# Query, key and value projections of a gated block's second attention as three fp32r products; value copies on ScalarE; the last batch's weight transfers at other places

## The reference, cut to what matters

```python
q = (src @ Wq + bq).reshape(B, T, N_HEAD, HEAD_DIM)
k = (src @ Wk + bk).reshape(B, T, N_HEAD, HEAD_DIM)
v = (src @ Wv + bv).reshape(B, T, N_HEAD, HEAD_DIM)
scores = jnp.einsum('bqhd,bkhd->bhqk', q, k) * scale
probs = jax.nn.softmax(scores, axis=-1)
attn = jnp.einsum('bhqk,bkhd->bqhd', probs, v).reshape(B, T, D_MODEL)
attn = attn @ Wo + bo
x = _layer_norm(src + attn, ln1_g, ln1_b)
...
    h = jax.nn.relu(x @ W1[e] + b1[e])
    y = h @ W2[e] + b2[e]
```

## Time and profile before

| | us |
|---|---|
| median of three runs | 532.24 |
| lowest and highest | 523.12, 532.72 |
| the profiled execution | 519.03 |
| its span | 517.2 |
| mean granted clock of TensorE | 0.963 |

### The profile page before, as it was taken

How to read it: one execution, slowest core, us unless ns; L and a number is a source line. 1 busy time by engine, 2 the same in 40 slices (tenths; PEclk the granted TensorE clock), 3 DMA queues, 4 the chain that set the end, 5 groups by cost and what they waited for, 6 DMA issues and landing times. The chain is left out here.

```text
span 517.2 us, 8461 instructions
## 1 busy us (share of the span) xinstructions
PE 467.6 (90%) x2595; PEld 271.6 (53%) x2595; DVE 382.4 (74%) x835; ACT 249.3 (48%) x499; POOL 211.2 (41%) x286
## 2 busy tenths in 40 slices
PE   3989999999999999999998698999979999999980
PEld 2545443344344345344343233325469999999980
DVE  4554879788878989878979779934778766666661
ACT  2112206657453657344646555678145555555540
POOL 4254303312004412604401453854367556656652
PEclk9999999999998999998999979889999999999995
DMA  8628740752284652341763592011121211121220
GB/s 232 130 89 261 173 95 3 247 198 60 73 143 98 214 174 77 120 121 53 194 202 100 184 182 82 3 45 41 42 81 30 70 62 62 52 63 54 68 61 11
DMA packets 39854, 54.99 MB, mean 106 GB/s; under 512 B 12413, under 2 KB 24203, under 8 KB 39820
## 3 DMA queue, kind: packets, MB, share of 16 engines
q1 hardware_dynamic: 34096, 38.18, 28.0%
q0 software_dynamic: 5232, 15.93, 9.6%
q10 hardware_dynamic: 492, 0.47, 0.3%
HBM read 36.73 MB, written 17.83 MB: 105 GB/s over the span
## 5 line engine op out<-in xcount | busy, mean ns | idle before, releaser
L776 DVE TENSOR_REDUCE mx<-amax 128x1 f32<-128x512 f32 x256 | 166.1, 678 | 41.3 <-PE amax L934 41.1
L630 ACT ACTIVATE probs<-sc 128x512 f32<-128x512 f32 x232 | 128.7, 596 | 135.3 <-PE sc L946 132.7
L934 PE MATMUL amax<-KS,QS 48*128 48x512 f32 x256 | 101.8, 474 | 4.1 <-DVE mx L776 2.8
L946 PE MATMUL sc<-QS,KS 50*128 50x512 f32 x232 | 91.1, 465 | 12.4 <-ACT probs L630 8.2
L946 PEld LDWEIGHTS sc<-QS,KS 50*128 50x128 f32 x232 | 36.8, 189 | 99.1 <-ACT probs L630 51.4
L934 PEld LDWEIGHTS amax<-KS,QS 48*128 48x128 f32 x256 | 40.6, 188 | 21.5 <-DVE mx L776 14.6
L1379 PE MATMUL amax<-W_hi,hid_hi 128*128 128x256 f32 x160 | 46.1, 288 | 0.0
L1379 PE MATMUL amax<-W_lo,hid_hi 128*128 128x256 f32 x160 | 45.2, 283 | 0.0
L1379 PE MATMUL amax<-W_hi,hid_lo 128*128 128x256 f32 x160 | 45.2, 283 | 0.0
L556 POOL TENSOR_TENSOR an<-av,rec 128x256 f32<-128x256 f32 x16 | 10.2, 636 | 83.7 <-DVE rec L765 83.6
L1095 POOL DMA_INDIRECT out_dram<-slot_z,ids_now x22 | 27.3, 1240 | 28.9 <-DVE slot_z L1299 24.4
(11 more groups left out here) (264 smaller groups left out, 932.1 us busy)
## 6 DMA issues: line engine op xcount, KB each, us to landing
qk_dram<-HL SPq DMA_DIRECT2D x16, 512.0 KB, 4.5
QS<-qk_dram SPq DMA_DIRECT2D x90, 64.0 KB, 3.0
KS<-qk_dram SPq DMA_DIRECT2D x90, 64.0 KB, 2.9
W_sb<-in_L_ffn_W SPq DMA_DIRECT2D x8, 512.0 KB, 4.2
xc<-in_x SPq DMA_DIRECT2D x4, 512.0 KB, 3.5
xc<-in_ctx SPq DMA_DIRECT2D x4, 512.0 KB, 4.5
tok_dram<-xc POOLq DMA_DIRECT2D x4, 512.0 KB, 3.6
res_dram<-t_a POOLq DMA_DIRECT2D x4, 512.0 KB, 3.9
```

Of the source, the lines that this page charges most:

```text
L630: nc.scalar.activation(probs[:, n % 8, c * 512:(c + 1) * 512], score_bank(u)[:, :], ACT.Exp, scale=SCALE).then_inc(exp_done, 1)
L776: nc.vector.reduce_max(mx[:, to:to + 1], amax[m % 3][:, :], AX.X).then_inc(max_done, 1)
L934: nc.tensor.matmul(amax[m % 3][:, :], QS[rows, pair, chunk * P:(chunk + 1) * P], KS[rows, pair, :], start=True, stop=True).then_inc(A_full, 1)
L946: nc.tensor.matmul(score_bank(u)[:, :], KS[rows, pair, kc * P:(kc + 1) * P], QS[rows, pair, :], start=True, stop=True).then_inc(sc_full, 1)
```

## The change

- **Three products.** Wq, Wk and Wv are split once, in the lead-in: ScalarE writes three fp32r high halves `qkv_hi` ahead of xT, POOL six low halves `qkv_lo` behind `scale(0)`. `srcT` becomes fp32r, and VectorE writes `srcT_lo` from the transposes' bank, which is held until then (`sl_done`). A block of q or k is six fp32r matmuls of 512 columns, three per half; a half of v is six of 256 columns. The second half of q waits for `srcT_lo`.
- **Value copies.** ScalarE copies v into V1 without a bias. Since the probabilities of a query sum to one, the value bias is taken through Wo once and added to the row Bo: Bv is loaded in head order by four small DMAs on ScalarE's queue, transposed on TensorE, copied by ScalarE, multiplied with Wo in two matmuls and added by VectorE, all in the lead-in. POOL's first `residual` waits for it.
- **Loads.** Wq, Wk, Wv go ahead of the rows for all partitions, of which seven are left. `qkv_hi` and `srcT_lo` share memory with the W1 pieces of experts 2 and 3, which are therefore loaded once the last v is done; both tables of pieces get new units.
- **POOL.** Each low half of `split_early` is written as four quarters. In batches 0 and 1 the store of the expert input and the load of the next residual stand at units 125 and 130 in place of right behind the arithmetic.

```diff
+            with ExitStack() as shared:
+                shared.enter_context(nc.sbuf_tensor("W1_first", [P, 4, F], fp32))
+                srcT_lo = shared.enter_context(nc.sbuf_tensor("srcT_lo", [P, KD, S], fp32r))
+                qkv_hi = shared.enter_context(nc.sbuf_tensor("qkv_hi", [P, 3 * KD, D], fp32r))
             W1_sb = att("W1_sb", [P, E * KD, F])
...
-                 -44: ("q", 0), -41: ("q", 1), -39: ("k", 0), -36: ("k", 1)}
+                 -44: ("q", 0), -41: ("q", 1), -39: ("k", 0), -36: ("k", 1), -33: ("v", 0), -31: ("v", 1)}
...
-                  -43: (("q", 0),), -40: (("q", 1),), -38: (("k", 0),), -35: (("k", 1),), -33: (("v", 0),), -31: (("v", 1),),
+                  -48: (("sT", 0),), -47: (("sT", 1),), -43: (("q", 0),), -40: (("q", 1),), -38: (("k", 0),), -35: (("k", 1),),
...
-        GPSIMD = {-98: "ln0", -90: "bias", -59: "ln1", -53: "x1", -47: "residual", 80: "ln2", 113: "xf"}
+        GPSIMD = {-98: "ln0", -90: "bias", -59: "ln1", -53: "x1", -47: "residual", 80: "ln2", 113: "xf", 125: "xf_store", 130: "xf_next"}
...
-        FIRST_LAYERS = {14 + 14 * i: i for i in range(E * KD)}
+        FIRST_LAYERS = {14: 0, 28: 1, 42: 2, 56: 3, 211: 4, 216: 5, 229: 6, 233: 7}
...
-        SECOND_LAYERS = {144 + 10 * i: i for i in range(2 * E)}
+        SECOND_LAYERS = {144: 0, 147: 1, 197: 2, 206: 3, 221: 4, 225: 5, 237: 6, 241: 7}
...
-            for i, v in ((BO2, Bo), (BV, Bv), (G1, ln1_g), (B1, ln1_b), (RW, router_w.rearrange("d o -> (d o)")), (G2, ln2_g), (B2, ln2_b)):
+            for n, ap in (("Wq", Wq), ("Wk", Wk), ("Wv", Wv)):
+                load_weight(n, ap, qkv_loaded)
+            for i, v in ((BO2, Bo), (G1, ln1_g), (B1, ln1_b), (RW, router_w.rearrange("d o -> (d o)")), (G2, ln2_g), (B2, ln2_b)):
...
             scale(0)
+            for w in range(3):
+                pool.wait_ge(qkv_high, w + 1)
+                for k in range(KD):
+                    j = KD * w + k
+                    nc.gpsimd.tensor_tensor(qkv_lo[:, j, :], w_second[:, j, :], qkv_hi[:, j, :].bitcast(fp32), ALU.subtract).then_inc(qkv_split, 1)
             bias(0)
...
-                nc.gpsimd.tensor_tensor(low, whole, high.bitcast(fp32), ALU.subtract).then_inc(early_split, 1)
+                pool.wait_ge(early_split, 5 * EARLY.index((w, part)) + 1)
+                for q in range(4):
+                    low_q, whole_q, high_q = [quarter(t, q) for t in (low, whole, high)]
+                    nc.gpsimd.tensor_tensor(low_q, whole_q, high_q.bitcast(fp32), ALU.subtract).then_inc(early_split, 1)
...
+                elif task == "v":
+                    act.wait_ge(v_full, b * 2 + i + 1)
+                    nc.scalar.activation(V1[b % 2][:, 2 * i:2 * i + 2, :, 0:DH], bank[:, :].rearrange("p (t h d) -> p t h d", t=2, h=H), ACT.Identity).then_inc(v_done, 1)
...
+                if (task, i) == ("xT", 0):
+                    act.wait_ge(qkv_loaded, 3 * 16)
+                    for w in range(3):
+                        nc.scalar.activation(qkv_hi[:, KD * w:KD * (w + 1), :], w_second[:, KD * w:KD * (w + 1), :], ACT.Identity).then_inc(qkv_high, 1)
...
+                elif task == "sT":
+                    dve.wait_ge(sT_done, b * 2 + i + 1)
+                    nc.vector.tensor_tensor(srcT_lo[:, i, :], bank[:, :], srcT[:, i, :].bitcast(fp32), ALU.subtract).then_inc(sl_done, 1)
...
-                elif task == "v":
-                    dve.wait_ge(v_full, b * 2 + i + 1)
-                    nc.vector.tensor_tensor(V1[b % 2][:, 2 * i:2 * i + 2, :, 0:DH], bank[:, :].rearrange("p (t h d) -> p t h d", t=2, h=H),
-                                            rows_bc[:, BV:BV + 1, :].rearrange("p o (h d) -> p o h d", h=H).broadcast_to([P, 2, H, DH]), ALU.add).then_inc(v_done, 1)
...
+            for c in range(KD):
+                side_work("sT", c, 0)
+            dve.wait_ge(vb_full, 1)
+            nc.vector.tensor_tensor(rows_bc[:, BO2, :], BANKS[0][:, 0:D], rows_bc[:, BO2, :], ALU.add).then_inc(vb_done, 1)
             for v in V1:
                 nc.vector.memset(v[:, :, :, DH:2 * DH], 1.0).then_inc(v1_ready, 1)
...
+            def parts_features(bank, w, c, half, full):
+
+                steps = [(0, 0, 0), (0, 0, 1), (1, 0, 0), (1, 0, 1), (0, 1, 0), (0, 1, 1)]
+                for wp, xp, k in steps[3 * half:3 * half + 3]:
+                    last = nc.tensor.matmul(bank[:, :], w[wp][:, k, c * P:(c + 1) * P], (srcT, srcT_lo)[xp][:, k, :], start=((wp, xp, k) == steps[0]), stop=((wp, xp, k) == steps[-1]))
+                if half == 1:
+                    last.then_inc(full, 1)
...
-                    pe.wait_ge(sT_done, b * 2 + 2)
-                    features_out(bank, w_sb["W" + task], i, srcT, half, qk_full)
+                    pe.wait_ge((sT_done, sl_done)[half], b * 2 + 2)
+                    parts_features(bank, qkv_parts[task], i, half, qk_full)
```

100 lines of the change are left out of this document (73 added, 27 removed).

## The result

The changed kernel takes 546.57 us, the median of four runs (545.4 to 551.92); the kernel before took 527.68 us in the same rounds (522.97 to 532.72). The ratio is 1.047 with a 95% interval of 1.035 to 1.059: slower. (Ratios leave out every run more than 1.5% above the fastest of its kernel, so they are not the quotients of the medians.) I had said 521 us.

What follows compares the result with a forecast made beforehand. TensorE was taken to bound the projection stretches, with VectorE having little to spare. Lead-in +2.2, projections -4.4, last batch -3.2 and quarters 0 sum to -5.4 us, from 526.8 to 521 us; range 508 to 533.

Steps and rivals of the forecast that it cites:

- rival (d): Projections beside attention: short TensorE idle times bring eight more low-clock stretches, +8.2 us, 535 us; chance 0.15.
- The products: Projections on TensorE: fp32r products save 0.20 us per q or k half, 0.14 per v half, 2.2 us per batch.
- Rival (b): Projections: weight loads of the new products are not hidden, +2.2 instead of -4.4 us, 528 us; chance 0.08.
- VectorE swaps two value copies ... I take two thirds, 4.4 us: Projections of batches 1 to 3: VectorE will be late, so 4.4 of 6.6 us are gained, ends 2.0 and 6.6.
- The lead-in: Before the first scores: later xT and low half of q lose 2.2 us, ends 0 and 4.
- Rival (c): Lead-in: Wv lands at 22 us and projections come late, sum +0.6 us, 527 us; chance 0.08.
- The last batch: Last batch's transfers: no large load ahead of the maxima gains 3.2 us, ends 0 and 4.8.
- SP writes the maxima out at 289.51, behind ... a 512 KB load: Last batch: maxima wait behind twelve stack loads and a 512 KB load on SP; 4.4 us hang on it.
- nobody waits for POOL then: First two batches: moving POOL's store and residual load apart makes them wait 3.4 us at most, effect 0.
- ScalarE's copies: Projections: two more ScalarE evictions of about 0.60 us per batch cost nothing; 3.6 us lost if cover is gone.
- The quarters: POOL's low halves of weight splits written as four quarters: effect 0, ends -1.5 and +1.5 us.
- rival (a): Whole kernel: all gains come through and three low-clock stretches go, -16.5 us, 510 us; chance 0.17.

Runs made afterwards that it cites:

- e13: e10 with two W2 loads moved from units 171 and 173 to 187 and 188, and a third from 197 to 202: 529.5 us, ratio 1.004.
- e16: e13 with the products in fp32 of the high halves: 533.9 us, ratio 1.012.
- e1: The changed kernel with the three fp32r products replaced by one fp32 product of the high halves: 537.2 us, ratio 1.011.
- e10: The changed kernel with e5's lead-in, e9's wait on POOL, some KS loads issued earlier and three weight loads moved: 532.3 us, ratio 1.007.
- e5: The changed kernel with high halves made behind xT and gates, POOL's first bias ahead of its low halves, ScalarE's QS moves later: 539.0 us, 1.015 by the medians.
- e4: The kernel before with only the change's moved weight loads and their semaphore: 528.5 us, ratio 1.000.
- e9: The kernel before with POOL's FFN input store of batches 0 and 1 held until maxima two batches on are back in QS: 532.7 us, ratio 0.999.
- e17: e13 with the value copies on VectorE again, without the bias: 531.0 us, ratio 1.007.
- e18: e16 without VectorE's low halves of srcT and TensorE's wait for them: 531.6 us, ratio 1.003.
- e7: The kernel before with the second product of each q and k block over 256 of its 512 columns: 533.8 us, ratio 0.998.
- e11: The kernel before with the change's moved weight loads and e10's three edits to the transfers, not the lead-in: 537.3 us, ratio 1.024.

## Why the prediction was wrong

The forecast failed, and what came has rival (d)'s sign but not its mechanism. (d) had short idle times between the groups of products; what came is two waits of over 3 us for a transfer, a longer lead-in, and a clock that fell behind these and at other places as well. Its 8.2 us for eight more low stretches were too few: the changed kernel has 55 us more at the low clock, sixteen times 3.4.

**The products** were the right size: 0.79 us a half of q or k in place of 0.955 (1.58 and 1.91 for two), 0.81 in place of 0.96 for v, so 8 x 0.165 + 4 x 0.15 = 1.9 us a batch against my 2.2. (My 0.66 and 0.86 for a half were both too short, so the difference held.) Even the 4.4 us that I took for them is what e13 has over e16, in a kernel whose transfers had first been moved; that the number agrees is luck, since my two thirds were for VectorE's being late. Rival (b), loads that are not hidden, is refuted by the rows from 275.12 us.

**The step that failed** is "VectorE swaps two value copies ... I take two thirds, 4.4 us": I asked only whether TensorE or VectorE would bound the shorter stretch, and not what was timed against it. The way of k over DRAM was: q and k evicted, stored, landed, fetched in six loads, all paced by SP, VectorE and ScalarE, with the v blocks and four scores as its cover. In the earlier trace rows nothing shows it, nor do the waits at a batch's first maxima, because it was just covered. In the changed kernel the cover fell short by 3.65 and 3.31 us, idle time in which the clock dropped, and undoing the products alone gains 9.4 us in the medians (e1) and 3.6% by the ratios: the term has the wrong sign, and is off by some 14 us or more. That the short products do save where these waits are gone (e10, e13) shows that the step failed by the overlap and not by the products' price.

**The lead-in** (2.2, ends 0 to 4) cost 4.9 us in the profile, and e5 gives back some 7.6 by the medians. Wv landed near the late end of my range (xT at 19.00, I had said 17.8), the cover was 0.4 us and not 0.7, and I did not price the low clock behind TensorE's idle 2.83 us, 1.7 more: these two are the steps that failed here. My 0.4 us for the low half of q was right: 5.4 us late in all (41.86), of which srcT is 5.0. Rival (c), a landing at 22 us, did not happen.

**The last batch** (3.2, ends 0 to 4.8) is worth 0, give or take some 2.5 us (e4). The step that failed is "SP writes the maxima out at 289.51, behind ... a 512 KB load": I looked at SP's queue alone, and what slowed it was POOL's store at 288.85 us. I had even costed that store's move at 0, "nobody waits for POOL then", which was true of POOL and not of what it sends. And with the delay gone (e9) the time did not move, so the 4.4 us that I hung on it were too many as well. In the changed kernel the wait is still there, 2.81 us.

**ScalarE's copies** at 0 hold as far as e17 can tell. VectorE's low halves, which I had at nothing of their own, may cost up to some 5 us (e18). **The quarters** at 0 were not tried alone.

**The clock.** I gave (d) 0.15 because idle times of 0.45 us stand all over the last batches at full clock. Those were the wrong idle times to look at. What I had in the earlier trace rows was the right one: 2.42 us without work, and 6.8 us at 1.2 GHz behind it. My range began at 508, below rival (a)'s own 510, and ended at 533, short of (d)'s 535: the upper end is where more room was needed. The Trainium skill, TensorE: Matmul & The Clock Gate, section HAM oscillation — how this bites in real kernels, tells of a kernel whose clock fell after each wait for a DMA; the rows at 22.30 us here (where TensorE waited for ScalarE, and that for Wv) and those of e7 agree with it, while 44 of the 75 us at the low clock in the changed kernel, and 17 of e13's 44, follow no such wait and show that it is not all. Why the clock falls there stays open.

## What to carry to other kernels

Before making an engine faster, list what runs beside its work and ends just in time: a transfer that shows no wait in the profile may have next to nothing to spare (here about 0.1 us, by the estimate above). Measure from its issue to its first use, and shorten that way before the work that covers it. Idle times of TensorE like those here, 1.4 to 3.7 us for a transfer, cost more than themselves where the granted clock falls behind them, as it mostly did here; price both. And a late transfer is to be looked for in all queues: a unit number in an engine's own order is no time, and a move in it does nothing unless something in between makes the engine wait.

## What I had not expected of the hardware

Two loads of 512 KB ahead of the maxima's way out, which takes 2.0 us alone, make it 6.7 (6.73 in e10, 6.76 in e11), and a 512 KB store or load on another engine's queue, issued 0.1 to 1.3 us ahead, makes it 3.0 to 4.1 (3.04 and 3.13 in the changed kernel, 3.59 and 3.92 before, 4.07 in e4). TensorE may stay at the low clock for 44 us on end while it is busy for 40.96 of them (e7, from 281.20), in the changed kernel for 23.9 us with no idle time at all (from 343.10), in e10 for 27 (from 326.15): being at work did not bring the clock back there. And the unchanged kernel spreads over 523 to 541 us, so that these runs cannot tell a part worth under 3 us.
